# Two-layer graph attention and mixture-of-experts network: the combining of expert rows moved into the preparation of the second attention

## The reference, cut to what matters

```
x = x + _L0_ffn_ref(_layernorm(x), ...)     # two experts of 16 for each row
#   moe = sum(topk_w * sel)                 # the two experts' rows, weighted
#   y = layernorm(x) + moe
#   (y - mean(y)) / sqrt(var(y) + eps) * gamma + beta
x = x + _L1_gnn_ref(_layernorm(x), adj, adj, ...)
#   qkv = x @ Wqkv + bqkv                   # then scores, softmax, product with v
```

## Time and profile before

| what | value |
|---|---|
| median of 3 runs | 2739.37 us (2734.53 to 2739.38) |
| the profiled execution's own time | 2733.8 us |
| its span in the trace | 2732.0 us |
| PE busy | 2485.0 us, 91% |
| DVE busy | 2026.6 us, 74% |
| ACT busy | 1612.4 us, 59% |
| POOL busy | 1481.3 us, 54% |

### The profile page before, as it was taken

The page is one execution under the profiler, slowest core; times in us unless marked ns, Lnnn a source line. Parts: engine busy times, 40 slices in busy tenths (PEclk is TensorE's granted clock), DMA queues, the critical chain, the costliest instruction groups (busy, mean ns, idle before and its releaser), DMA issues. The chain is left out here.

```text
span 2732.0 us, 59677 instructions
## 1 busy us (share of the span) xinstructions
PE 2485.0 (91%) x20186; PEld 2025.9 (74%) x20187; DVE 2026.6 (74%) x4258; ACT 1612.4 (59%) x3050; POOL 1481.3 (54%) x1747
## 2 busy tenths in 40 slices
PE   6799999999974999096999999999779999999999
PEld 5377777777764999074777777777568888888888
DVE  5899989899955444687777777777667777777776
ACT  1577777777740333144666666666467777777775
POOL 6477667766632555432211112211288888888886
PEclk9799999999985999598999999999889999999999
DMA  2011111111135222210111111111000000000001
GB/s 98 21 42 42 63 43 42 43 43 45 40 130 201 70 70 67 92 55 27 42 58 44 41 41 41 41 43 39 7 1 0 0 0 0 0 0 0 0 0 41
DMA packets 43884, 114.23 MB, mean 42 GB/s; under 512 B 5621, under 2 KB 29918, under 8 KB 37982
## 3 DMA queue, kind: packets, MB, share of 16 engines
q1 hardware_dynamic: 38174, 97.16, 10.1%
q0 software_dynamic: 5568, 15.21, 1.8%
HBM read 99.21 MB, written 13.15 MB: 41 GB/s over the span
## 5 line engine op out<-in xcount | busy, mean ns | idle before, releaser
L2143 PE MATMUL f_pm<-f_wl,f_yt 128*128 128x256 f32 x2640 | 625.7, 380 | 0.0
L2143 PEld LDWEIGHTS f_pm<-f_wl,f_yt 128*128 128x128 f32 x2640 | 477.8, 191 | 51.1
L1087 POOL TENSOR_TENSOR ADJ<-ADJ,a_off 128x2708 f32<-128x2708 f32 x22 | 131.1, 5959 | 543.1 <-DVE ADJ L1166 543.1
L544 POOL TENSOR_SCALAR a_off<-ADJ 128x677 bf16<-128x677 f32 x84 | 275.0, 3296 | 224.2 <-DMA ADJ<-in_adj 209.6
L118 POOL TENSOR_SCALAR f_yy<-f_th,f_rs 128x255 f32<-128x255 f32 x660 | 367.0, 570 | 21.8 <-POOL f_rs L113 21.8
L521 ACT COPY a_wt<-a_tp 128x512 f32<-128x512 f32 x528 | 256.3, 565 | 173.0 <-PE a_tp L730 172.8
L1993 DVE SCALAR_TENSOR_TENSOR f_gg<-f_th,f_pm 128x512 f32<-128x512 f32 x319 | 219.1, 687 | 176.7 <-ACT f_th L2087 175.7
L621 DVE SCALAR_TENSOR_TENSOR a_lg<-a_f1s,F2S,a_fo 128x1024 f32<-128x1024 f32 (+1 forms) x264 | 289.7, 1150 | 28.8 <-issue 22.7
L1146 DVE CUSTOM_DVE_ANT_0 a_sc<-a_qk,ADJ 128x1024 f32<-128x1024 f32 (+1 forms) x264 | 288.3, 1093 | 30.4 <-PE a_qk L1244 30.4
L2087 ACT ACTIVATE f_th<-f_pm 128x512 f32<-128x512 f32 x319 | 190.5, 597 | 199.9 <-PE f_pm L2143 199.9
L1110 ACT ACTIVATE a_sc<-a_sc,a_mx 128x1024 f32<-128x1024 f32 (+1 forms) x264 | 277.7, 1052 | 45.2 <-DVE a_mx L1151 45.2
(11 more groups left out here) (295 smaller groups left out, 4604.9 us busy)
## 6 DMA issues: line engine op xcount, KB each, us to landing
ADJ<-in_adj SPq DMA_DIRECT2D x44, 1354.0 KB, 5.8
W<-in_L_ffn_w SPq DMA_DIRECT2D x32, 512.0 KB, 9.6
m_got<-YD SPq DMA_DIRECT2D x6, 768.0 KB, 10.7
out<-X SPq DMA_DIRECT2D x21, 128.0 KB
X<-in_x SPq DMA_DIRECT2D x3, 768.0 KB, 9.8
XD<-XF SPq DMA_DIRECT2D x3, 768.0 KB
m_b<-in_L_ffn_b SPq DMA_DIRECT2D x1, 2048.0 KB, 7.6
m_rows<-XD,SLOT POOLq DMA_INDIRECT x58
```

The lines of the kernel that those rows point to most:

```text
L544: pool.tensor_scalar(off[:, b, cols], adj[:, b, cols], 0.0, HUGE, ALU.is_equal, ALU.mult).then_inc(off_done[b], 1)
L2143: mm = pe.matmul(out, yt[:, g, r, k, :], wl[:, k, :], start=(k == 0), stop=(k == KD - 1))
```

## The change

`moe_combine` goes away, and its work moves into `layer1_prepare`. Both are now done over five batches `MERGED` of 1, 2, 3, 3 and 2 pairs. The normalized rows are not kept in SBUF: they are read again from XD, a third stream beside the two of YD. `got` holds two batches of up to 6 tiles, and the load of batch k waits until ACT has read batch k - 2. The gamma product is done in place on POOL instead of on DVE. The statistics of X are taken batch by batch, without a loop. GW is kept until then. Per batch k, the lists are now as follows.

- DVE: combine batch k + 1, statistics of X for batch k, results of batch k - 1.
- POOL: scale and shift of the expert rows of batch k + 1, then the second normalization of batch k, then gamma product and addition to X for batch k + 1.
- ACT: `z` of batch k + 1, then for each pair i of batch k the copy of pair i + 1 and the bias and rounding of pair i.
- PE: as before.

```diff
+MERGED = [(0, 1), (1, 3), (3, 6), (6, 9), (9, NPAIR)]
 def layer1_prepare(nc, io, keep, layer1):
...
+        got = ph.sb("got", [P, 2, TOPK + 1, most, D])
+        z = ph.sb("z", [P, 4, D])
...
         def _(sp):
+            def load(k):
+                t0, t1 = 2 * MERGED[k][0], 2 * MERGED[k][1]
+                whole = min(t1, NT - 1)
+                if k >= 2:
+                    for t in tiles_of(k - 2):
+                        sp.wait_ge(z_done[t % 4], t // 4 + 1)
+                for r, (rows, first_row) in enumerate((("YD", 1), ("YD", 1 + N), ("XD", 1))):
+                    sp.dma_start(got[:, k % 2, r, 0:whole - t0, :], keep[rows][
+                        first_row + P * t0:first_row + P * whole, :].rearrange("(t p) d -> p t d", p=P)
+                        ).then_inc(loaded[k], 16)
...
+            load(0)
+            sp.dma_start(gamma[:, :], bcast_rows(io["L0_ffn_gamma"], P)).then_inc(g_in, 16)
+            load(1)
             sp.dma_start(wqkv[:, :, :], io["L1_gnn_Wqkv"].rearrange("(k p) o -> p k o", p=P)).then_inc(w_in, 16)
...
+            for k in range(2, len(MERGED)):
+                load(k)
             first_adj(sp, io, layer1["ADJ1"], layer1["adj_in"])
...
         def _(pool):
...
+            def residual(k):
+                for t in tiles_of(k):
+                    r = slice(t % 4, t % 4 + 1)
+                    pool.wait_ge(z_done[t % 4], t // 4 + 1)
+                    pool.tensor_tensor(z[:, r, :], z[:, r, :], gamma[:, :].rearrange("p (a d) -> p a d", a=1),
+                                       ALU.mult).then_inc(zz_done[t % 4], 1)
+                    pool.wait_ge(zz_done[t % 4], t // 4 + 1)
+                    pool.tensor_tensor(X[:, t:t + 1, :], X[:, t:t + 1, :], z[:, r, :], ALU.add).then_inc(x_out[t % 4], 1)
+
+            def normal(k):
+                a, end = MERGED[k]
+                pool.wait_ge(x_moments, k + 1)
+                inverse_deviation(pool, xmom, xrs, neg_half, 2 * a, 2 * end, x_pchain, 3 * k).then_inc(x_inv, 1)
+                pool.wait_ge(x_inv, k + 1)
+                for t in tiles_of(k):
+                    i, b = divmod(t, 2)
+                    if i >= 2:
+                        pool.wait_ge(turned, i - 1)
+                    standard_rows(pool, xn[:, t % 4:t % 4 + 1, :], X[:, t:t + 1, :], xrs, t).then_inc(xn_done[b], 1)
+            expert_deviation(0)
+            pool.wait_ge(g_in, 16)
+            residual(0)
+            for k in range(len(MERGED)):
+                if k + 1 < len(MERGED):
+                    expert_deviation(k + 1)
+                normal(k)
+                if k + 1 < len(MERGED):
+                    residual(k + 1)
...
         def _(dve):
...
+            combine(0)
+            for k in range(len(MERGED)):
+                if k + 1 < len(MERGED):
+                    combine(k + 1)
+                row_stats(k)
+                if k == 0:
+                    dve.wait_ge(b_in, 32)
+                else:
+                    results(k - 1)
+            results(len(MERGED) - 1)
...
-            turned_out(0)
-            for i in range(NPAIR):
-                if i < NPAIR - 1:
-                    turned_out(i + 1)
-                full_out(i)
+            standard(0)
+            for k in range(len(MERGED)):
+                if k + 1 < len(MERGED):
+                    standard(k + 1)
...
+                for i in range(*MERGED[k]):
+                    if i < NPAIR - 1:
+                        turned_out(i + 1)
+                    full_out(i)
```

## The result

The changed kernel takes 2748.59 us (median of 8 runs, 2745.46 to 2750.91), the kernel before 2737.3 (median of 8 runs, 2734.31 to 2740.8): 11.3 us more, a ratio of 1.0041 with a 95% interval of 1.003 to 1.0052. The profiled execution took 2750.91 us with a span of 2749.1. Its phase began 3.6 us later than before, behind code that is the same, and another 1.1 us lie behind the phase. So I compare the stretch from SP's first load of expert rows to DVE's last instruction of the phase, and beside it medians.

A forecast was written before the change was run, and what follows sets the result against it. DVE, nearly full in two successive chains, was to bound the joined phase: 95.6 + 9.7 + 19.5 + 20.6 = 145.4 us against 136.8, 8.6 longer, so 2748.0 us (range 2730 to 2758).

The forecast's parts named there:

- DVE's own work: DVE's list in the joined phase: combining 25.1, moments 5.8, statistics of X 7.3, results 57.4, in sum 95.6 us.
- the holds: POOL's instructions slow DVE's in the joined phase: 17.6 us on terms and copies, 3 for normalizations, in sum 20.6.
- 0.85 x 0.47: Share of POOL's 44 two-input instructions meeting a DVE term or copy, times us lost by DVE at each meeting: 17.6 us.
- Waits for data: DVE waits for rows from HBM in the first three batches: 5.1, 1.9 and 2.7 us, in sum 9.7.
- Hand-off: At batch borders DVE waits for a pair behind the next batch's first: 12.5, about 7, then nothing; sum 19.5 us.
- The sum: Whole joined stretch: 124.8 + 20.6 = 145.4 us against 136.8, 8.6 longer, so a median of 2748.0 us.
- Rival, copies not held: POOL doesn't slow DVE's copies, only the 44 terms pay, about 10 us: stretch 138.8, time 2741; chance 0.22.
- Rival, POOL's work costs nothing: POOL's work falls into DVE's waits and beside its one-input work: stretch 128.8, 8 less, time 2731; chance 0.15.
- Rival, PE stays slow: PE's clock stays at 0.50 after standing still, a pair takes near 11 us: 11 us more, time 2759; chance 0.11.

The follow-up runs named there:

- e9: e1 with the whole addition to X on DVE, two instructions per tile replacing ACT's z and POOL's product and addition, YD asked for earlier: 2732.3 us.
- e2: The changed kernel without the gamma product, so POOL has 22 two-input instructions instead of 44: 2740.1 us, ratio 1.0014 to the kernel before.
- e6: The changed kernel with POOL's gamma product made twice, once into a tile nobody reads: 2756.2 us, ratio 1.0079 to the kernel before.
- e1: The changed kernel, with PE and ACT finishing the last pair of batches 0 and 1 before turning the next batch's first pair: 2728.2 us, ratio 0.9970.
- e10: e9 with all copies of `high` on ACT for pairs 0 to 7 and two for the last three: 2726.8 us, ratio 0.9961.
- e5: The changed kernel with a one-input scale and shift of the same size in place of POOL's gamma product: 2744.3 us, ratio 1.0030.
- e3: The changed kernel with the gamma product on DVE, three tiles ahead of the statistics of X: 2746.0 us, ratio 1.0031 to the kernel before.

## Why the prediction was right, step by step

- **DVE's own work (95.6) and the holds (20.6)** make 116.2. Measured: 149.1 less 32.9 of waits, 116.2. That both are 116.2 is partly luck, but the parts are near too. e9 splits it: its stretch less its waits is 117.3; less 44 new instructions at 0.40 it is 99.7. If this rest is the same in the changed kernel, which has PE's and ACT's other order, POOL's two-input instructions cost 16.5 (I had 17.6), and 4.1 stand over the 95.6, where I had 3 for the normalizations. My 0.85 x 0.47 = 0.40 for an instruction is what e2 (0.40) and e6 (0.38) show. The two factors weren't measured apart.
- **Waits for data**: 9.7 predicted, 10.9 measured. Batch 1 was the most mis-sized of the three: 3.6 instead of 1.9, batch 2 1.7 instead of 2.7, the first 5.7 instead of 5.1. Two steps of my working don't follow from its own costs: at 370 GB/s batch 1 would be there at 9.3 and not at 9.8, and DVE's list from there to the end of the first statistics of X is 6.5 us, not 8.5. In the trace that piece took 7.6, holds included. I had counted the rows at 370 GB/s; the transfers of gamma, weights and biases that SP issues among them were left out. That they cause it wasn't tested.
- **Hand-off**: 19.5 predicted (12.5, 7, 0), 22.0 measured (12.9, 7.9, and 1.2 in two short ones later): the largest error of the sum. e1 shows the mechanism.
- **The sum**: a stretch of 145.4 predicted, 149.1 measured; all of the 3.7 lies in the waits. The median came out at 2748.6 against 2748.0, and that close is luck: I had forecast 8.6 us more than before, the medians differ by 11.3, and the kernel before was 2 us below the median that I had started from.
- **Rival, copies not held** (2741): falls. They were held as hard as the terms. The Trainium skill, SBUF — State Buffer, section "Who interferes with whom", says that copies in the two-port modes contend with GpSimd. These copies do contend (53.0 us instead of 37.8); in which mode they run no trace shows. It says too that the loser blocks for the whole instruction. Charged in full for each of the 22 products, that would make e2 22 x 0.72 = 16 us faster; it was 8.8. This speaks against the full charge for each instruction, not against blocking: the held copies of pair 0 take 0.77 us, as long as one instruction of POOL there, and less the 0.28 to 0.30 that a copy takes anyway that is a loss of 0.47 to 0.49.
- **Rival, POOL's work costs nothing** (2731): falls. POOL's products lay outside DVE's waits, for the reason that stood against it, and e2 and e6 give their price. Its time, though, is about what e1 has, by taking away the other term.
- **Rival, PE stays slow** (2759): the clock was low (0.64 and 0.74 in the two waits, 0.87 behind them), but behind its two long waits DVE waited for `high` only 1.2 us in all.

## What to carry to other kernels

When two chains are joined on the engine that is nearly full in both, add up that engine's list first, then look at each border of a batch for the engine that does the next batch's work before this batch's last, and for what waits behind the full engine's list (in e10, PE waited 6.9 us for DVE to take v). An instruction moved to GpSimd isn't gone from VectorE while both read SBUF: here 0.40 us of each 0.72 came back, and the product was worth about the same on either engine. The order of TensorE and ScalarE at two borders was worth 19 to 20 us, more than the whole change; the copies on ScalarE gave 2 more in the median, which these intervals don't tell from none.

## What the runs showed of the hardware that I had not expected

- GpSimd's one-input instructions hold VectorE as well: 0.19 to 0.24 us for each of e5's 22, the larger part of it in the terms, which read two inputs. The 16-bit copies (512 numbers in 0.28 us) are held too: two of them took 1.06 us instead of 0.60 beside the normalizations of the changed kernel. I had priced this only for the normalizations, at 3 us in all. The statistics, with one input, are not held (0.412 in the mean beside everything).
- What had begun first kept its length: VectorE's `low`, begun 0.55 us before GpSimd's product, took its usual 1.23 us, and the product 1.26 instead of 0.72, at three places. The prediction had this direction only for the normalizations.
- It depends on the order of the lists who meets whom: in e3 the additions ran beside products and statistics, and the terms kept 0.474 us, their length alone, where they took 0.55 and 0.57 in the changed kernel.
